# Splitting made weight blocks one tile later in a fused FFN, attention, FFN kernel, and normalising rows two at a time

## The reference

```python
x = x + 0.5 * ffn(layernorm(x))      # x: (2, 1024, 512) float32
x = x + attention(layernorm(x))      # one head of 128, sequence 1024, with biases
x = x + 0.5 * ffn(layernorm(x))      # the same FFN weights
# ffn(x) = (silu(x @ Wg) * (x @ Wu)) @ Wd, inner width 1376
# Wg, Wu (512 x 1376), Wd (1376 x 512): 4-bit, unpacked as scale[g, n] * (w4 - (z4[g, n] + 1))
```

## Time and profile before

| | us |
|---|---|
| median of 3 runs (lowest, highest) | 912.73 (910.3, 912.78) |
| the profiled execution's own time | 910.43 |
| its span, first to last instruction | 908.6 |
| TensorE busy | 848.4 (93%), mean granted clock 0.979 |
| VectorE busy | 509.2 (56%) |
| ScalarE busy | 269.0 (30%) |
| GpSimd busy | 263.9 (29%) |

### The profile page before, as it was taken

How to read it: one execution, slowest core, us unless ns; L and a number is a source line. 1 busy time by engine, 2 the same in 40 slices (tenths; PEclk the granted TensorE clock), 3 DMA queues, 4 the chain that set the end, 5 groups by cost and what they waited for, 6 DMA issues and landing times.

```text
span 908.6 us, 10687 instructions
## 1 busy us (share of the span) xinstructions
PE 848.4 (93%) x4040; PEld 685.8 (75%) x4040; DVE 509.2 (56%) x830; ACT 269.0 (30%) x459; POOL 263.9 (29%) x221
## 2 busy tenths in 40 slices
PE   5999999775999999999999895999999999999998
PEld 4677678553778888888888784688887878888876
DVE  6777754744475454454877866554544754444442
ACT  3323221233431222142564474112212511221221
POOL 5434324554210415120225164115331111111100
PEclk9999999988999999999999898999999999999999
DMA  5665455323546544332315126744444244444221
GB/s 132 181 210 175 133 174 190 129 105 133 214 155 239 161 135 144 106 109 71 113 52 176 52 82 238 248 162 140 142 138 149 107 138 163 153 134 153 61 92 47
DMA packets 65711, 128.09 MB, mean 141 GB/s; under 512 B 22956, under 2 KB 33884, under 8 KB 60540
## 3 DMA queue, kind: packets, MB, share of 16 engines
q1 hardware_dynamic: 64348, 125.64, 41.3%
q10 hardware_dynamic: 1152, 1.36, 0.5%
q0 software_dynamic: 160, 0.42, 0.2%
HBM read 94.91 MB, written 32.31 MB: 140 GB/s over the span
## 4 chain that ended last, share of the span: by engine, by line
PE 78%; DVE 8%; POOL 6%; issue 3%; ACT 2%; DMA 1%; SPq 0%; DVEq 0%; POOLq 0%; ACTq 0%
PE ps L666 39%; PE ps L659 34%; PE ps L677 2%; POOL t L1891 2%; DVE t L1446 2%; POOL t L1917 1%; POOL t L1921 1%; DVE t L1449 1%; PE ps L1052 1%; DVE xn L1478 1%; DMA shift<-in_shifts 1%; DVE wi L1446 1%; PE ps L748 1%; DVE wf L1564 1%; ACT xn L1136 1%
## 5 line engine op out<-in xcount | busy, mean ns | idle before, releaser
L659 PE MATMUL ps<-blk,ring 128*128 128x512 f32 (+1 forms) x1386 | 323.2, 391 | 11.2 <-POOL blk L1891 7.7
L659 PEld LDWEIGHTS ps<-blk,ring 128*128 128x128 f32 (+1 forms) x1386 | 257.1, 186 | 71.3 <-POOL blk L1891 8.8
L666 PE MATMUL ps<-wd,hT 128*128 128x512 f32 (+1 forms) x1056 | 253.4, 394 | 8.7 <-DVE h L1619 6.5
L666 PEld LDWEIGHTS ps<-wd,hT 128*128 128x128 f32 (+1 forms) x1056 | 198.3, 189 | 52.6 <-DVE h L1619 6.3
L1936 POOL TENSOR_TENSOR h<-h,u 128x512 f32<-128x512 f32 (+1 forms) x33 | 42.7, 1293 | 327.1 <-ACT h L1243 327.1
L666 PE MATMUL ps<-xT,wp 128*128 128x512 f32 x480 | 120.6, 405 | 11.3 <-DVE h L1619 10.5
L666 PEld LDWEIGHTS ps<-xT,wp 128*128 128x128 f32 x480 | 90.5, 193 | 35.7 <-DVE h L1619 12.6
L1449 DVE TENSOR_TENSOR u<-ps,p1s 128x512 f32<-128x512 f32 (+1 forms) x66 | 45.3, 687 | 99.1 <-PE ps L659 99.1
L1243 ACT ACTIVATE h<-h 128x512 f32<-128x512 f32 (+1 forms) x33 | 20.9, 632 | 178.4 <-DVE h L1449 178.4
L1449 DVE TENSOR_TENSOR h<-ps,p1s 128x512 f32<-128x512 f32 (+1 forms) x33 | 22.8, 691 | 66.1 <-PE ps L659 66.1
L1449 DVE TENSOR_TENSOR u<-ps,u 128x512 f32<-128x512 f32 (+1 forms) x66 | 45.6, 691 | 23.3 <-PE ps L659 22.2
(11 more groups left out here) (137 smaller groups left out, 930.7 us busy)
## 6 DMA issues: line engine op xcount, KB each, us to landing
ring<-wsaved SPq DMA_DIRECT2D x30, 1024.0 KB, 5.1
ring<-wsaved SPq DMA_DIRECT2D x33, 768.0 KB, 4.4
wsaved<-wp SPq DMA_DIRECT2D x10, 1024.0 KB, 3.9
stream<-xres SPq DMA_DIRECT2D x32, 256.0 KB, 2.4
xn<-stream SPq DMA_DIRECT2D x8, 1024.0 KB, 7.5
xres<-stream SPq DMA_DIRECT2D x32, 256.0 KB, 3.4
wsaved<-wp SPq DMA_DIRECT2D x10, 512.0 KB, 3.0
xres<-in_L_attn_x SPq DMA_DIRECT2D x16, 256.0 KB, 3.6
```

Of the source, the lines that this page charges most:

```text
L659: mm = pe.matmul(ps[0:w, bank, :], ring[:, slot, which, a, kt, 0:w], blk[:, which, b, kt, :], start=not onto and kt == 0 and n == 0, stop= ...
L666: mm = pe.matmul(bank_ap, lhs(a), rhs(b), start=first and n == 0, stop=last and n == 2)
```

## The change

ScalarE makes the high halves of made tile i - 1 behind Silu(i), and the last behind the loop. VectorE makes the low half of its two blocks of tile i - 1 between h(i) and the three differences of tile i, and the last behind the loop. GpSimd's work on the blocks is the same. Statistics come in two visits of two row tiles for each group, at i = 1, 2 and 4, 5; variances at 2 and 5; shifts at 4 and 7; the powers before j = 3 and 6; ScalarE's application in visits of two at i = 5, 6 and 8, 9. VectorE's two early hidden low halves move to i = 4 and 5.

```diff
@@ ScalarE
-            def ln_apply(t):
+            def ln_apply(t, tiles=range(RT)):
                 act.wait_ge(s_nmr, {0: 1, 2: 2, 3: 3}[t])
-                for r in range(RT):
+                for r in tiles:
@@ ScalarE, plain_bottom
                     act.activation(hidden(i)[0:w, :], ps[0:w, plain_bank(1, i, 0), :], ACT.Silu).then_inc(s_silu, 1)
-                    t_blocks_hi(i)
-                    if i == 5:
-                        ln_apply(2)
-                    if i == 7:
-                        ln_apply(3)
+
+                    if i:
+                        t_blocks_hi(i - 1)
+                    if i in (5, 6, 8, 9):
+                        ln_apply(2 if i < 7 else 3, (0, 1) if i in (5, 8) else (2, 3))
                     if i in (3, 4):
                         plain_hi(1, i - 3)
+                t_blocks_hi(NT - 1)
@@ VectorE
-            def ln_stats(t):
+            def ln_stats(t, tiles=range(RT)):
                 if t:
                     dve.wait_ge(d_row[t], 16)
-                for r in range(RT):
+                for r in tiles:
@@ VectorE, first_blocks
                 minus(t, t, b[:, 0:4:2, 1, :, :]).then_inc(s_t13, 1)
+
+            def first_blocks_lo(j):
+                i = T_ORDER[j]
+                t = fp32_t(t13, i)
                 dve.wait_ge(s_th13, j + 1)
                 minus(t_blocks(i)[:, 0:4:2, 1, :, :], t, f32(t_blocks(i))[:, 0:4:2, 0, :, :]).then_inc(s_tlo13, 1)
@@ VectorE, plain_bottom
+                    if i:
+                        first_blocks_lo(i - 1)
                     first_blocks(i)
-                    if i in (2, 4):
-                        ln_stats(1 + i // 2)
-                    if i in (3, 5):
-                        ln_var(1 + i // 2)
-                    if i in (4, 6):
-                        ln_shift(i // 2)
-                    if i in (3, 4):
-                        plain_lo(1, i - 3)
+                    if i in (1, 2, 4, 5):
+                        ln_stats(2 if i < 3 else 3, (0, 1) if i in (1, 4) else (2, 3))
+                    if i in (2, 5):
+                        ln_var(2 if i < 3 else 3)
+                    if i in (4, 7):
+                        ln_shift(2 if i < 5 else 3)
+                    if i in (4, 5):
+                        plain_lo(1, i - 4)
+                first_blocks_lo(NT - 1)
@@ GpSimd
             for j in range(NT):
-                if j in (4, 6):
-                    deviation(j // 2)
+                if j in (3, 6):
+                    deviation(j // 3 + 1)
                 second_blocks(j)
```

## The result

The changed kernel takes 898.0 us (median of 4 runs, 896.21 to 900.99) against 911.67 us for the kernel before beside it; the ratio is 0.9854 with an interval of 0.982 to 0.9888. The forecast was 897.5 us. The profiled execution took 897.0 us, its span 895.2 us, 13.4 us less than before.

The account below looks back on a forecast made before the run. The bound was TensorE's 22.7 us idle, set by a ring of waits through VectorE, ScalarE and GpSimd; GpSimd ending 15.2 us earlier, less 1.2 us for clock, gave 14.0 us: 897.5 us forecast, range 889 to 904 us.

Parts of the forecast that it names:

- The ring (part 1): VectorE, ScalarE and GpSimd wait in turn, 8.56 us a tile; ScalarE's later split spreads this over two, 4.3 us each.
- GpSimd's pace (parts 2, 3, 5): GpSimd sets the tile pace: 5.55 us alone, 6.6 us with VectorE exchanges, plus 2.2 us for its two powers.
- The start and the end (part 6): GpSimd starts tile 1 at 149.6 us; behind the last tile, 3.5 us to the end of its fourth operation.
- The rows (part 4): Pair 1's rows normalised two at a time, ScalarE pieces of 1.45 us hidden: nothing charged, up to 1.3 us in range.
- TensorE's clock: Charge of 1.2 us for TensorE's clock, taken off the 15.2 us gain to leave 14.0 us.
- the rival on the clock: Clock stays down, TensorE sets 7.15 us a tile: gain 10 to 12 us, 899 to 902 us; chance 0.12.
- the mark: Start of down tile 2 on TensorE, at 232.46 us before: what moves it moves the kernel's end one for one.
- VectorE's half (part 3): Low half one tile later on VectorE: its 0.70 us wait per tile goes, but exchanges cost GpSimd 0.34 us each.
- The sign I gave for TensorE: TensorE's idle time on the successor of the VectorE product h falls from 22.7 us to 7 to 9.
- Whole-instruction lock: Second instruction starts only once the first ends: tiles 7.4 to 8.0 us, 903 to 909 us; chance 0.13.
- Collision-free: VectorE's turns fall into GpSimd's gaps: 5.55 to 6.1 us a tile, 888 to 893 us; chance 0.13.
- The slower rival: GpSimd stops for each whole VectorE operation and restarts: 9.0 us a tile, 917 to 919 us; chance 0.04.

Follow-up runs that it names:

- early-hidden kernel: Changed kernel with hidden tile 2 split at i = 5 and 6, tiles 3 and 4 ahead of the last made tile's halves: 891.2 us.
- bank operand: Changed kernel with the second operand of VectorE's four block operations read from a PSUM bank instead of SBUF, weights not the reference's: 886.4 us.

## Why the prediction was right, point by point

**The ring (part 1).** Right, and it is all of the gain: ScalarE's half alone gives it, and with it taken back the kernel is slower than before.

**GpSimd's pace (parts 2, 3, 5).** Forecast 6.6 us a tile and 2.2 us for the powers, 61.6 us for nine tiles; measured 212.76 - 151.12 = 61.6 us, of which the powers are 2.5, so 6.57 us a tile. Single tiles differ more, from 5.9 to 7.3 us without the powers; the forecast is right on the mean. The price of an exchange was read from one meeting each way, 1.15 us a pair, and measures 1.14. The powers measure 1.7 (stage) to 2.6 us (median).

**The start and the end (part 6).** GpSimd started tile 1 at 151.12 us, not 149.6; the later start of the whole stage, 1.6 us, is all of that. From there to the end of the fourth operation of tile 10 it took 65.1 us, forecast 65.1. Sized rightly, but read as if nothing could be done: the early-hidden kernel shows that this end need not be on the path.

**The rows (part 4).** Nothing was charged, and nothing shows in the time: with rows in fours the kernel took 896.9 us, in twos 898.0. The pieces do delay Silu: the last, 1.50 us from 204.40 us on, stands ahead of Silu at 205.81 us, and TensorE waits 2.90 us for the h behind it. But down tile 2 waits for GpSimd's last tile all the same.

**TensorE's clock.** I took 1.2 us for it and pointed to the rival on the clock in the tiles. In the tiles there was no loss (grant 1.00 to 199 us); it came behind the mark. From down tile 2 to pair 1's first product took 28.23 us before and takes 29.57: 1.34 us, 36 matmuls in 9.82 in place of 8.48 us. Right in size, wrong in place, and since the prediction gives no working for its 1.2 us, the size is luck. The account closes: 15.3 us earlier at the mark, 1.6 us for the later start, 1.3 us for the clock, and from pair 1 on 646.8 against 647.9 us, together 13.4 us.

**VectorE's half (part 3).** This is the step that failed, inside a right sum. I wrote that its 0.70 us wait per tile goes, as if that were part of the gain. That wait lay beside GpSimd's own work and cost nothing. Moving the low half makes it and the three differences meet GpSimd's half-size operations more: 39.4 us for the half-size operations against 36.3 with the low half in its old place. That is 3.1 us of the 9.8 us by which the half-size operations exceed forty times 0.74 us; the other 6.7 us are there with ScalarE's half alone. My 6.6 us tile holds the cost, but I did not see that this edit made a third of it and gave nothing back.

**The sign I gave for TensorE.** "7 to 9 us" of idle time was wrong: 7.4 us stand before h, but 5.6 more before the split of tile 2. Taking the whole gain off the idle time, 22.7 - 15.2 = 7.5 us, gives such a number, and it leaves no room for quicker matmuls. 13.0 us of idle and 15.3 us of gain fit since TensorE's matmuls are also quicker: its busy time to down tile 2 is 82.9 - 13.0 = 69.9 us, before it was 98.1 - 23.3 = 74.8 us (23.3 with the small gaps), on the same instructions. So TensorE got back 4.9 us up to the mark. Before, 24 matmuls took 7.15 us behind a longer gap; now they take 5.7 to 5.8 us in every tile. The prediction had the clock only as a cost; its sum came right because it follows GpSimd and not TensorE.

**The other signs.** 27 of the 40 half-size operations took over 1.0 us, VectorE's differences 1.01 us on average, and down tile 2 started at 218.8 us, which is 217.2 without the later start: all as forecast.

**Rivals.** Whole-instruction lock: the second of a pair ends 0.56 or 0.58 us behind the first, not 0.69 and 0.74, and tiles are 6.57 us apart without the powers, not 7.4 to 8.0. Clock: the tiles' 24 matmuls took 5.7 to 5.8 us, not 7.15. Collision-free: its time, 888 to 893 us, lies a little above what the bank operand gave (886.4 us): priced about rightly, but the collisions are there. The slower rival did not come for the changed kernel. The kernel with VectorE's half alone was slower than before, by another way than mine: no stopped GpSimd, but a longer ring.

## What to carry to other kernels

When three in-order queues form a ring, ask of each instruction that moves whether it leaves the ring or enters it. Letting the copy that waits for the slow engine fall one tile behind the work that TensorE needs broke this ring; moving the low half on VectorE as well only placed it where it cost. Before putting two engines side by side, look in the old trace for the few places where they already meet: one meeting each way priced an exchange here to 0.01 us, and all exchanges together cost 11.6 us.

## What the runs showed of the hardware

An operation of VectorE with one SBUF input can be held up too. The timeline of VectorE in the changed kernel, two statistics and a small tensor_scalar, all with one SBUF tensor:

```profile
176.47 1.27 DVE L1458 BATCH_NORM_STATS2 stats<-xn 128x6 f32<-128x512 f32 x2
...
178.19 1.02 DVE L1468 TENSOR_SCALAR rstd<-mv 128x4 f32<-128x4 f32 x1
```

The same instruction took 0.17 us at 159.27 us, where an operation of GpSimd ended 0.04 us after its start and the next began at 159.39 us; here it ended at 179.21 us, when GpSimd's operation of 177.89 us had ended at 179.19. It is no single case: with ScalarE's half alone it took 0.61 us from 159.42 us and 0.59 us from 180.16 us, and ended 0.03 us behind GpSimd's operation both times. The statistics ran beside GpSimd's at their usual 1.27 us. The Trainium skill, SBUF — State Buffer, section "Who interferes with whom", names tensor_scalar among the operations that can take the shared port pair in a two-port mode; the rows agree that it is held up, and no run shows the mode itself. The same section lets the second instruction block for the whole of the first: by the rows of the two-input operations it gets through 0.13 to 0.16 us of its own time meanwhile (0.69 - 0.56, 0.74 - 0.58).
